# A two-layer graph network on one core: the first chunk's rounding, the edge lists and two early waits rearranged

## What is computed

```python
h = (x @ W).reshape(n, heads, out_ch)
e = leaky_relu(alpha_src[src] + alpha_dst[dst], 0.2)      # alpha = sum(h * a) per node
p = exp(e - segment_max(e, dst)[dst])
out = segment_sum(h[src] * p / segment_sum(p, dst)[dst], dst) + b
# block 0: h = elu(gat(x, 8 heads)); out = gat(h, 1 head); x = layernorm(x + out)
# block 1: relu and layer norm after the first, residual products Wr1, Wr2
```

## Time and profile before

| | |
|---|---|
| median of 3 runs | 365.04 us |
| the profiled execution's own time | 364.43 us |
| its span | 362.6 us |
| PE busy | 349.9 us (96%) |
| DVE, ACT, POOL busy | 213.9, 218.5, 242.5 us |
| HBM read | 64.15 MB |

### The profile page before, as it was taken

The page is one execution under the profiler, slowest core; times in us unless marked ns, Lnnn a source line. Parts: engine busy times, 40 slices in busy tenths (PEclk is TensorE's granted clock), DMA queues, the critical chain, the costliest instruction groups (busy, mean ns, idle before and its releaser), DMA issues.

```text
span 362.6 us, 6075 instructions
## 1 busy us (share of the span) xinstructions
PE 349.9 (96%) x2058; PEld 299.1 (82%) x2060; DVE 213.9 (59%) x544; ACT 218.5 (60%) x375; POOL 242.5 (67%) x163
## 2 busy tenths in 40 slices
PE   8999899999999999999999999999999999999994
PEld 4888788888988988988898898898677787788883
DVE  4998864445427327344542832637687767953776
ACT  4995668646745854764775585475476667264601
POOL 2389648784793965779479396574258589687911
PEclk9999999999999999999999999999999999999999
DMA  7988948566646547555664764666072654437002
GB/s 234 302 297 238 398 163 252 183 179 171 198 155 222 163 140 243 162 193 174 174 194 156 217 169 141 251 167 223 5 248 95 209 153 123 161 104 240 6 2 87
DMA packets 24544, 65.15 MB, mean 180 GB/s; under 512 B 1952, under 2 KB 3024, under 8 KB 24528
## 3 DMA queue, kind: packets, MB, share of 16 engines
q1 hardware_dynamic: 20864, 55.02, 46.0%
q10 hardware_dynamic: 3664, 9.92, 10.4%
HBM read 64.15 MB, written 0.79 MB: 179 GB/s over the span
## 4 chain that ended last, share of the span: by engine, by line
PE 78%; DVE 12%; ACT 6%; DMA 2%; issue 1%; ACTq 0%; DVEq 0%
PE ps L985 57%; PE ps L1070 8%; PE ps L1274 5%; PE ps L1104 2%; ACT e L757 1%; DMA b_rows<-in_L_gnn_b 1%; PE ps L1049 1%; DVE e L1491 1%; DVE ps L1544 1%; PE ps L1166 1%; DMA raw<-in_L_gnn_W 1%; ACT ring_hi L357 1%; DVE ps L1554 1%; DVE ps L1628 1%; PE ps L1338 1%
## 5 line engine op out<-in xcount | busy, mean ns | idle before, releaser
L370 POOL TENSOR_TENSOR ring_lo<-raw,ring_hi 128x768 fp32r<-128x768 f32 x92 | 167.0, 1854 | 74.6 <-ACT ring_hi L357 74.6
L357 ACT ACTIVATE ring_hi<-raw 128x768 fp32r<-128x768 f32 x96 | 77.3, 840 | 34.9 <-PE ps L985 28.9
L386 POOL TENSOR_TENSOR ring_lo<-raw,ring_hi 128x512 fp32r<-128x512 f32 (+1 forms) x40 | 59.5, 1519 | 22.5 <-ACT ring_hi L379 22.4
L985 PE MATMUL ps<-ring_hi,zT_hi 128*128 128x256 f32 (+1 forms) x256 | 69.3, 346 | 0.7 <-ACT zT_hi L799 0.7
L985 PE MATMUL ps<-ring_lo,zT_hi 128*128 128x256 f32 (+1 forms) x256 | 67.1, 337 | 0.0
L985 PE MATMUL ps<-ring_hi,zT_lo 128*128 128x256 f32 (+1 forms) x256 | 66.8, 338 | 0.0
L1491 DVE CUSTOM_DVE_ANT_0 e<-ps,att 128x768 f32<-128x768 f32 x38 | 34.3, 957 | 47.5 <-PE ps L985 47.5
L985 PE MATMUL ps<-ring_hi,xT_hi 128*128 128x512 f32 x192 | 51.2, 342 | 0.0
L985 PE MATMUL ps<-ring_lo,xT_hi 128*128 128x512 f32 x192 | 50.0, 336 | 0.0
L985 PE MATMUL ps<-ring_hi,xT_lo 128*128 128x512 f32 x192 | 49.8, 337 | 0.0
L985 PEld LDWEIGHTS ps<-ring_lo,zT_hi 128*128 128x128 f32 x256 | 43.0, 188 | 5.7
(11 more groups left out here) (172 smaller groups left out, 546.9 us busy)
## 6 DMA issues: line engine op xcount, KB each, us to landing
raw<-in_L_gnn_W SPq DMA_DIRECT2D x54, 768.0 KB, 4.5
raw<-in_L_gnn_Wr SPq DMA_DIRECT2D x8, 768.0 KB, 4.3
att<-in_L_gnn_a_src ACTq DMA_DIRECT2D x10, 384.0 KB, 4.0
att<-in_L_gnn_a_dst ACTq DMA_DIRECT2D x10, 384.0 KB, 5.4
raw<-in_L_gnn_W SPq DMA_DIRECT2D x4, 384.0 KB, 5.2
x_sb<-in_x SPq DMA_DIRECT2D x3, 256.0 KB, 5.1
rows_hc<-in_L_gnn_b SPq DMA_DIRECT2D x1, 512.0 KB, 7.9
rows_hc<-in_L_gnn_g SPq DMA_DIRECT2D x1, 512.0 KB, 8.7
```

Source lines behind the costliest of these rows:

```text
L357: eng.activation(slot_hi(c), raw_chunk(c), ACT.Copy).then_inc(hi_done, 1)
L370: eng.tensor_tensor(slot_lo(c), raw_chunk(c), slot_hi(c).bitcast(F32), ALU.subtract)\
L386: eng.tensor_tensor(ring_lo[:, q["ring_at"]:q["ring_at"] + w], raw[:, q["raw_group"], q["raw_at"]:q["raw_at"] + w], ring_hi[:, q["ring_at" ...
L985: last = pe.matmul(ps[:, at + to:at + to + hi - lo], a, b[:, lo:hi], start=start and n == 0 and to != D, stop=stop and n == PASSES - 1, sk ...
```

## The change

x's first part and both edge lists are issued by ACT, at its very start, before its first activation; SP's queue has three transfers fewer. The edge lists land as rows (64 partitions of 128 numbers, so an edge list is stored in another order, which the counts do not depend on). DVE converts them, PE transposes them ahead of chunk 0's third pass, and DVE copies them out of PSUM. x's first two column blocks are transposed into two banks and rounded one by one; the two matmuls on zeros behind them are gone; chunks 0 and 2 are done pass by pass over both tiles, with the wait for the weights' low part only before the second. x's third part goes to the place of the first, after a wait. ACT copies the count sums before it issues the attention vectors and splits two chunks; far is made tile by tile, each followed by that tile's tops, and ACT's copy of the counts waits for both. For head 1, PE's scores wait for the second low part of z instead of the third, and DVE waits for the third before it writes masked scores. ACT rounds tile 0 of head 1's features inside elu(0), does head 1's leaks ahead of the splits of chunks 4 and 5 of phase 2, and orders them: leaks, chunk 4, tile 1's rounding, exps, chunk 5.

```diff
@@ storage
-        edges = sb("edges", [P, 2, ET], I32)
+        edge_rows = sb("edge_rows", [2 * ET, P], I32)
+        edge_rows_f = sb("edge_rows_f", [2 * ET, P])
-        XT_AT = 0
+        XT_AT = [0, BANK, 2 * BANK, 2 * BANK + N, 0, N]
+        EDGES_AT = S_AT + N + 2 * ET
...
@@ SP, ACT
+        def load_x(eng, b):
+            cols = slice(2 * b * P, (2 * b + 2) * P)
+            eng.dma_start(x_sb[:, :, cols], x.rearrange("(t p) c -> p t c", p=P)[:, :, cols])\
+               .then_inc(x_loaded[b], 16)
...
             sp.dma_start(raw[:, 0, 0:D], w1[:, 0, 0, :]).then_inc(single_loaded[0], 16)
-            load_x(0)
-            sp.dma_start(edges[:, 0, :], src.rearrange("(p t) -> p t", p=P)).then_inc(edges_loaded, 16)
-            sp.dma_start(edges[:, 1, :], dst.rearrange("(p t) -> p t", p=P)).then_inc(edges_loaded, 16)
             sp.dma_start(raw[:, 0, D:2 * D], w1[:, 1, 0, :]).then_inc(raw_full[0], 16)
-            load_x(1)
+            load_x(sp, 1)
...
+            load_x(act, 0)
+            act.dma_start(edge_rows[0:ET, :], src.rearrange("(t p) -> t p", p=P)).then_inc(edges_loaded, 16)
+            act.dma_start(edge_rows[ET:2 * ET, :], dst.rearrange("(t p) -> t p", p=P)).then_inc(edges_loaded, 16)
             act.wait_ge(half_set, 1)
             act.activation(rstd[:, 0:1], half[:, :], ACT.Exp)
...
@@ -695,23 +699,24 @@
                 for t in range(first, end):
                     act.activation(step(t), iota[:, :], ACT.Sign, bias=src_bias[:, t:t + 1]).then_inc(step_act_done, 1)
 
-            def input_hi(b):
-                act.wait_ge(xT_ps, b + 1)
-                act.activation(xT_hi[:, 2 * b:2 * b + 2, :].rearrange("p k n -> p (k n)"),
-                               ps[:, XT_AT + b * BANK:XT_AT + (b + 1) * BANK], ACT.Copy).then_inc(xT_hi_done, 1)
+            def input_hi(first, chunks, at_done):
+                act.wait_ge(xT_ps, at_done)
+                act.activation(xT_hi[:, first:first + chunks, :].rearrange("p k n -> p (k n)"),
+                               ps[:, XT_AT[first]:XT_AT[first] + chunks * N], ACT.Copy).then_inc(xT_hi_done, 1)
 
             split_hi(act, FIRST_PHASE, 0, reused=False)
             act.dma_start(b1_rows[:, :], b0_b1.rearrange("(t p) -> t p", p=P)).then_inc(b1_loaded, 16)
-            input_hi(0)
+            input_hi(0, 1, 1)
+            input_hi(1, 1, 2)
             split_hi(act, FIRST_PHASE, 1, reused=False)
             act.wait_ge(iota_cast, 1)
             act.wait_ge(src_biased, 1)
             steps(0, 3)
             split_hi(act, FIRST_PHASE, 2, reused=False)
-            input_hi(1)
+            input_hi(2, 2, 3)
             steps(3, 5)
             split_hi(act, FIRST_PHASE, 3, reused=False)
-            input_hi(2)
+            input_hi(4, 2, 4)
             load_att(0, b0_as1[0:1, :], b0_ad1[0:1, :], D, reused=False)
             split_hi(act, FIRST_PHASE, 4, reused=False)
             split_hi(act, FIRST_PHASE, 5, reused=False)
@@ -726,6 +731,11 @@
                     act.wait_ge(a_dst_done, 2 * h + 2)
                 for i in range(NT):
                     projected_tile_hi(h, i)
+
+            def projected_after_dots(h, i):
+
+                act.wait_ge(a_dst_done, 2 * h + 2)
+                projected_tile_hi(h, i)
 
             def projected_tile_hi(h, i):
                 act.activation(feat(h_hi, h, i), source_at(h, i), ACT.Copy).then_inc(h_hi_done, 1)
@@ -791,6 +801,8 @@
                     act.wait_ge(elu_relu, 6 * h + 2 * q + 2)
                     pair = z[:, 2 * q * N:(2 * q + 2) * N]
                     act.activation(pair, pair, ACT.Exp, scale=-1.0).then_inc(elu_exp, 1)
+                if between is not None:
+                    between()
                 elu_hi(h, 2)
 
             def elu_hi(h, q):
@@ -810,6 +822,9 @@
                 leaks(h)
                 projected_hi(h)
                 exps(h, (1, 0))
+                after_exps(h, last)
+
+            def after_exps(h, last=False):
                 att_for(h + 1, last)
                 for c in range(4):
                     split_hi(act, 2 * h + 1, c)
@@ -834,12 +849,12 @@
             for c in (4, 5):
                 split_hi(act, 1, c)
             leaks(0)
+            act.wait_ge(counted, 1)
+            act.activation(step_sums, ps[:, STEPS_AT:STEPS_AT + 1 + N], ACT.Copy).then_inc(sums_copied, 1)
             att_for(1)
             for c in (0, 1):
                 split_hi(act, 2, c)
-            act.wait_ge(counted, 1)
-            act.activation(step_sums, ps[:, STEPS_AT:STEPS_AT + 1 + N], ACT.Copy).then_inc(sums_copied, 1)
-            act.wait_ge(far_done, 1)
+            act.wait_ge(far_done, NT)
             act.activation(counts[:, :, :].rearrange("p i n -> p (i n)"), ps[:, COUNT_AT:COUNT_AT + NT * N],
                            ACT.Copy).then_inc(counts_done, 1)
             exps(0, (1, 0))
@@ -847,10 +862,13 @@
                 split_hi(act, 2, c)
             weights_hi(0)
             act.wait_ge(b1_ready, 2)
-            elu(0)
+            elu(0, between=lambda: projected_after_dots(1, 0))
+            leaks(1)
             split_hi(act, 2, 4)
+            projected_after_dots(1, 1)
+            exps(1, (1, 0))
             split_hi(act, 2, 5)
-            softmax_and_elu(1)
+            after_exps(1)
             with act.Fori(2, H0 - 1) as h:
                 head(h)
             head(H0 - 1, last=True)
@@ -1125,14 +1143,16 @@
             pe.wait_ge(consts, 2)
             def transpose_x(b):
                 pe.wait_ge(x_loaded[b], 16)
+                if b == 2:
+                    pe.wait_ge(xT_lo_done, 1)
                 for k in (2 * b, 2 * b + 1):
                     for i in range(NT):
-                        at = XT_AT + k * N + i * P
+                        at = XT_AT[k] + i * P
                         last = pe.transpose(ps[:, at:at + P], x_sb[:, i, k * P:(k + 1) * P], ident[:, :])
-                last.then_inc(xT_ps, 1)
+                    if b == 0 or k % 2 == 1:
+                        last.then_inc(xT_ps, 1)
 
             transpose_x(0)
-            keep_warm(2, PROJ + 2 * BANK)
             for c in range(CH):
                 if c == 1:
                     pe.wait_ge(b1_loaded, 16)
@@ -1141,11 +1161,18 @@
                 if c in (1, 2):
                     transpose_x(c)
                 if c in (0, 2):
-                    pe.wait_ge(xT_hi_done, c // 2 + 1)
-                    chunk(FIRST_PHASE, c)
-                    for passes in (FIRST_TWO, LAST_ONE):
+                    pe.wait_ge(xT_hi_done, c + 1)
+                    pe.wait_ge(hi_done, c + 1)
+                    for passes in ((0,), (1,), LAST_ONE):
+                        if passes == (1,):
+                            chunk(FIRST_PHASE, c)
                         if passes is LAST_ONE:
                             pe.wait_ge(xT_lo_done, c // 2 + 1)
+                        if passes is LAST_ONE and c == 0:
+                            pe.wait_ge(edges_cast, 1)
+                            pe.wait_ge(iota_cast, 2)
+                            pe.transpose(ps[:, EDGES_AT:EDGES_AT + 2 * ET], edge_rows_f[:, :],
+                                         ident[0:2 * ET, 0:2 * ET]).then_inc(edges_ps, 1)
                         for i in range(NT):
                             last = product(ACC, i, node_tile(xT_hi, c, i), node_tile(xT_lo, c, i),
                                            slot_hi(c), slot_lo(c), c == 0, False, passes=passes)
@@ -1200,7 +1227,7 @@
             def rest_of_head(h, scores_at=1, first=0):
                 for c in range(first, CH):
                     if c == scores_at:
-                        pe.wait_ge(z_lo_done, 3 * h)
+                        pe.wait_ge(z_lo_done, 3 * h - 1 if first else 3 * h)
                         scores(h)
                     if c == 5:
                         weights(h)
@@ -1423,10 +1450,10 @@
         def _(dve):
 
             def input_lo(b):
-                dve.wait_ge(xT_hi_done, b + 1)
-                dve.tensor_tensor(xT_lo[:, 2 * b:2 * b + 2, :].rearrange("p k n -> p (k n)"),
-                                  ps[:, XT_AT + b * BANK:XT_AT + (b + 1) * BANK],
-                                  xT_hi[:, 2 * b:2 * b + 2, :].rearrange("p k n -> p (k n)").bitcast(F32),
+                dve.wait_ge(xT_hi_done, b + 2)
+                at, apart = XT_AT[2 * b], XT_AT[2 * b + 1] - XT_AT[2 * b]
+                of = ps[:, at:at + 2 * apart].rearrange("p (k n) -> p k n", k=2)[:, :, 0:N]
+                dve.tensor_tensor(xT_lo[:, 2 * b:2 * b + 2, :], of, xT_hi[:, 2 * b:2 * b + 2, :].bitcast(F32),
                                   ALU.subtract).then_inc(xT_lo_done, 1)
 
             dve.wait_ge(iota_ready, 1)
@@ -1439,10 +1466,13 @@
                        .then_inc(hot_done, 1)
 
             split_lo(dve, FIRST_PHASE, 0)
+            dve.wait_ge(edges_loaded, 32)
+            dve.tensor_copy(edge_rows_f[:, :], edge_rows[:, :]).then_inc(edges_cast, 1)
             input_lo(0)
```

(20 more changed lines are left out.)

12 lines of the change are left out of this document (5 added, 7 removed).

## The result

The changed kernel takes **367.06 us**, the median of 9 runs (366.42 to 368.48); before, in the same runs, 364.89 (9 runs, 364.45 to 365.65). The ratio is 1.0061, 95% interval 1.0046 to 1.0076: slower by 2.2 us, where 364.3 was forecast and 366.2 was the end of the range. The runs of after come in two groups, five from 366.42 to 367.06 and four from 368.35 to 368.48. The profiled execution, 368.35 us with a span of 366.2, is of the upper one.

The account below looks back on a forecast made before the run. TensorE is full from 60 to 200 us, so only its waits before 60 count. Count sums give 0.1, head 1's scores 0.6, start and transfers nothing: 0.7 off 365.04, forecast 364.3 us, range 363.2 to 366.2.

Parts of the forecast that it names:

- part 4: Head 1's scores and ACT's order: weights(1) at 56.4 instead of 57.00, 0.6 us gained; SP's later load costs nothing.
- the first paragraph's premise: Loop over the heads, 60 to 200 us: TensorE always busy, untouched by the change, so earlier gains or losses carry through.
- Rival (d): Head 1: its gain is given back by chunk 5's late low part or ACT waiting inside elu; 364.9, chance 0.07.
- a wait of ACT inside elu: Head 1: ACT waiting before the feature rounding moved inside elu, one of two ways to lose the 0.6 us gain.
- The tie on chunk 5's low part: Behind head 1's exps: low part ready after 3.45 us, PE wants it after 3.52; if late, up to 0.3 us.
- Rival (b): Front: b1's rows land at 12.3 instead of 9.38, PE 2.9 late; +1.8 us, 366.8, chance 0.18.
- Part 3: Count sums: chain on DVE starts 0.77 us sooner, tile order takes most back, 0.2 left; 0.1 in the sum.
- Part 1: First chunk: x's first part lands at about 4.3, first product 0.8 us sooner; nothing gained behind the counts' chain.
- The edges' way: Front: PE's added edge transpose costs 0.27 us and makes DVE's low part of chunk 1 0.1 to 0.3 us later.
- DVE's chain covers a gain of PE at the front: Before weights(0): DVE works without a break to 31.23, so the front's 0.4 us only becomes a longer wait.
- Part 2: Transfers at the front: b1's rows land at 9.1, the 768 KB load being issued after them; no gain or loss.
- rival (a): Front: b1's rows land at 10.5, PE 1.1 us late for chunk 1; gain cancelled, 365.0, chance 0.25.

Follow-up runs that it names:

- part 4 alone: Kernel before with only head 1's earlier scores and ACT's new order for head 1: 368.85 us (7 runs), ratio 1.0077.
- the start alone: Kernel before with only x's first part and edges issued by ACT, edges turned by PE, first chunk in passes, no zero matmuls behind x: 365.23 us, ratio 0.9998.
- the first mended kernel: Kernel before with sums copied sooner, far by tiles, head 1's new order, and elu(1) ahead of the late splits; old start: 364.08 us, ratio 0.9971.
- part 3 alone: Kernel before with only the count sums copied sooner and far made by tiles: 364.54 us (12 runs), ratio 0.9971.

## Why the prediction was wrong

**The step that failed** is the last sentence of part 4, which put SP's late load at nothing: "its chunks are the last two of the next projection, behind aggregate_T(1)". It asked when PE wants the chunks, and they are indeed not wanted early. It did not ask where ACT's splits of them stand: ahead of elu(1) in ACT's list. ACT runs its activations in order, so the late load held the relu, and the relu held PE. The size of the delay was nearly right: part 4's order makes the load 3.5 us later against weights(0), and some 3 were forecast. The price is 2.0 us in after, and 3.05 with the clock's 1.46 behind it in part 4 alone. The wait is at 68.89, so the first paragraph's premise, that the change touches nothing behind 60 us, fell with it.

No rival had this wait. Rival (d) had "a wait of ACT inside elu" at 0.6 us and a chance of 0.07, but its sign was ACT waiting before the rounding inside elu, that is before the feature rounding in elu(0), and after shows no wait there (at 49.00). The tie on chunk 5's low part, named beside it, did not show as a wait either. Rival (b) gave 366.8, near the measured 367.06, and that is luck: its b1's rows were to land at 12.3 and to hold PE, and they landed at 10.8 and decided nothing in after.

**Part 4's gain** was right: scores(1) run without a wait, and weights(1) came 1.93−1.32 = 0.61 sooner against weights(0); 0.6 was forecast.

**Part 3** was mis-sized, and its size is not one number. The sum had 0.2 for the chain, worked out from before's profile. With the leaks and maxima of that profile it is 0.39. The chain starts 0.88 sooner behind the maxima (0.67 instead of 1.55), and the tile order takes 0.5 of it: from the chain's first step to am it is 39.25−33.46 = 5.79 in after instead of 37.31−32.02 = 5.29. Where b1's rows are late, PE and the leaks are late with them, and it is 0.66. In after DVE is later still. There the old order would have started the chain 1.11 us behind the maxima (33.83−32.72 in the start alone), only 0.44 more than the new one, and the tile order takes as much again. So part 3 is worth nothing. The prediction priced parts 1 and 3 apart, but a late DVE takes away what part 3 gives.

**Part 1** had the sign wrong. x's first part was to land at 4.3 and landed at 5.7, taking 5.0 us instead of 3.6. The prediction had the Trainium skill, "DMA: Bandwidth & Descriptors", section "Issuing engines are not separate DMA queues", which says that transfers of different engines interleave on the same 16 DMA engines, and drew from it that the part gains its slot and nothing else. Between the two profiled executions it lost 0.9. Over all traces the loss is about half of that: with the old start x's first part lands at 4.8 to 5.3 in five traces, with the new one at 5.3 to 5.7 in nine. W1's first chunk lands later too (4.0 to 4.6, and 4.7 to 5.2), which agrees with the interleaving. In the new order x's part shares the time with W1's second chunk as well, issued at 1.18 instead of 2.63; which of the two chunks, or the edge lists, delays it was not separated.

The edges' way was costed as their transpose, 0.27, and "0.1 to 0.3 us later" on DVE. But the transpose stands behind two passes of chunk 0. DVE's low part of chunk 1 starts at 9.18 to 9.37 at the faster pace and at 10.67 to 11.04 at the slower one, against 8.19 to 8.96 in the five traces with the old start. So the term is some +0.9 or +2.4, against their median of 8.42. The forecast that DVE's chain covers a gain of PE at the front was sound: with b1's rows later in the first mended kernel, chunk 1 starts 1.2 us sooner and weights(0) no sooner (38.00, and 37.92). A loss on DVE itself is not covered.

**Part 2** took b1's rows at 9.1, because SP's 768 KB load would be held until behind them. SP issued it at 4.28, ahead of b1's rows, which came at 5.22 (with a split that waited for W1's first chunk) and landed at 10.8, near the 10.5 of rival (a). It did not decide in after, where PE reached that transpose at 10.84 anyway. In two executions at the faster pace it shows as 1.3 to 1.5 us of idleness (the row at 10.82 of the kernel with more warm-up, and 1.32 in that with the vectors behind weights_hi).

**Why the start is neutral on the median** and costs 1.9 at weights(0) between two profiles: before's profile is a good case of the old start. It has b1's rows turned at 9.43 and maxima at 30.47. Of the four other traces with the old start three have these rows landing at 10.3 to 10.5 and one at 9.7, and where PE waited for the later ones the maxima are at 31.27 and 31.37. The new start gives maxima at 31.33 at the faster pace (b1's rows turned later) and at 32.72 at the slower one (start alone). At the faster pace it so equals an execution of before with late rows, which fits the eight of twelve runs of the start alone around 365.1; the upper group, 1.2 us higher, has its one trace at the slower pace. That the paces make the groups in general is argued from these few traces, and the kernel with more warm-up, at the faster pace and in the upper group, shows that they are not the only cause. The prediction read a single execution, which lay 0.6 below its median, and did not ask which wait the difference was.

**Sum.** By medians the start and parts 3 and 4 alone give +0.1, −0.6 and +3.7, together 3.2; by the ratios −0.1, −1.1 and +2.8, together some 1.7. The whole change has 2.2 by either, so the sums are no finer than these intervals. The range failed by the one wait. Without it the change measures 365.05, inside it. That is still some 0.7 above the forecast. With the old start (364.08, the first mended kernel) the trace shows the gains of both parts.

## What to carry to other kernels

When a load comes later, look not only at who consumes the data, but at every engine that touches it in order on the way, and at what stands behind that touch in its list. A step that is moved can bring a transfer close behind one of a different queue, and then the transfer's length changes too. A gain on one engine's part of a chain lasts only while that engine is what the chain waits for, so price two changes together if both move the same chain. Before a loss or gain at the start is priced, ask which of the run times the profiled execution is one of.

## What the runs showed that was not expected

- **One line for two queues, in the middle of the kernel too.** The same 768 KB load took 4.7 us from issue to landing when the attention vectors were issued some 3 us ahead of it (after; 5.7 in part 4 alone) or behind it, and 7.1 and 7.4 us when they were issued 0.7 to 1.3 us ahead.
- **Issues overtake activations.** A transfer placed behind four activations without waits is issued before the first of them runs (55.85 against 55.99); placed behind one that waits for PE it came at 57.51. To delay a transfer here it took a wait, not work.
- **The clock after a pause.** After 3.05 us of idleness at 69.10 the granted clock was 0.51 for 3.3 us; after 2.56, 2.88 and 2.04 us at the same place PE's pairs kept their 0.51 us. After 1.46 us at the start, behind chunk 0, it was 0.50, though behind the 1.48 us of part 3 alone PE's pairs took 0.51 at once. The pause's length alone does not tell what it costs.
- **Two paces at the start.** The same instructions up to 9 us take either 1.09, 1.65 and 1.32 us or 0.63, 0.97 and 0.87, with a granted clock of 1.00 in both records. Of the traces with the new start, two of seven without extra warm-up have the faster pace and both with it do. The pause ahead of x's transposes does not decide it: 0.54 to 1.00 us at the slower pace, 0.66 to 0.84 at the faster. What does was not found, and two traces are too few to say that the warm-up helps.
